# An attention block and a routed expert block: matrix slices over eight batches, the last attention step in a new order, and the end in whole loads and halves

## The reference, cut to what matters

```python
x = x + _layernorm(_L0_attn_ref(_layernorm(x), Wq, Wk, Wv, Wo, gamma, beta))
x = x + _layernorm(_L0_ffn_ref(_layernorm(x), router_w, w1, w2))
...
probs = softmax(xt @ router_w)
top_p, top_i = top_k(probs, 2)
for e in range(8):
    gate_e = sum(where(top_i == e, top_p, 0.0))
    hidden = gelu(xt @ w1[e])
    out = out + gate_e[:, None] * (hidden @ w2[e])
```

## Time and profile before

| | |
|---|---|
| median of 3 runs | 724.96 us (724.06 to 725.15) |
| profiled execution | 728.19 us, span 726.4 us |
| PE busy | 685.2 us, 94% |
| DVE busy | 554.1 us, 76% |
| ACT busy | 520.7 us, 72% |
| POOL busy | 273.6 us, 38% |
| DMA | 34.88 MB |

### The profile page before, as it was taken

How to read it: one execution, slowest core, us unless ns; L and a number is a source line. 1 busy time by engine, 2 the same in 40 slices (tenths; PEclk the granted TensorE clock), 3 DMA queues, 4 the chain that set the end, 5 groups by cost and what they waited for, 6 DMA issues and landing times.

```text
span 726.4 us, 17681 instructions
## 1 busy us (share of the span) xinstructions
PE 685.2 (94%) x5954; PEld 592.6 (82%) x5955; DVE 554.1 (76%) x1914; ACT 520.7 (72%) x1687; POOL 273.6 (38%) x388
## 2 busy tenths in 40 slices
PE   4999999999999999999999999999989999999954
PEld 3788878888888888888888888888869989999921
DVE  5668889888898989888898989888896774444226
ACT  4787877887888778887788878888774665555415
POOL 3023534232323132332323232332313777655535
PEclk9999999999999999999999999999989999999978
DMA  9630000010000000000000000000020243322155
GB/s 160 205 80 8 9 9 16 17 30 10 23 9 24 9 24 12 22 23 17 23 9 24 9 23 12 20 24 9 17 69 20 71 124 112 90 79 79 39 190 171
DMA packets 43701, 34.88 MB, mean 48 GB/s; under 512 B 10624, under 2 KB 40320, under 8 KB 43616
## 3 DMA queue, kind: packets, MB, share of 16 engines
q1 hardware_dynamic: 37984, 23.81, 12.8%
q0 software_dynamic: 4544, 9.45, 3.6%
q10 hardware_dynamic: 1088, 0.54, 0.3%
HBM read 20.22 MB, written 13.56 MB: 47 GB/s over the span
## 4 chain that ended last, share of the span: by engine, by line
PE 78%; DVE 12%; DMA 3%; ACT 2%; issue 2%; DVEq 1%; POOL 1%; SPq 0%; POOLq 0%; ACTq 0%
PE PT1O L423 11%; PE M L683 9%; PE SC L406 8%; PE A L434 6%; PE M L385 5%; PE M L387 5%; PE M L386 5%; PE SC L414 4%; PE PT1O L442 3%; PE SC L409 3%; PE PT L447 3%; PE PT L446 3%; PE SC L385 3%; PE SC L386 2%; PE SC L387 2%
## 5 line engine op out<-in xcount | busy, mean ns | idle before, releaser
L1262 ACT ACTIVATE qk<-M 128x512 f32<-128x512 f32 x127 | 76.0, 599 | 84.5 <-PE M L387 84.5
L1273 ACT ACTIVATE prob<-SC,nmax 128x256 f32<-128x256 f32 x256 | 126.0, 492 | 0.0
L423 PE MATMUL PT1O<-pT,v_sb 128*64 128x256 f32 (+1 forms) x1024 | 98.6, 335 | 0.7 <-ACT pT L1278 0.7
L423 PEld LDWEIGHTS PT1O<-pT,v_sb 128*64 128x64 f32 x1024 | 64.0, 138 | 43.0 <-ACT pT L1278 17.4
L1267 ACT ACTIVATE prob<-SC,nmax 128x128 f32<-128x128 f32 x256 | 95.6, 383 | 3.4 <-DVE nmax L777 3.3
L1543 POOL DMA_INDIRECT expert_rows<-v_sb,got x78 | 76.8, 984 | 47.0 <-ACT v_sb L1417 25.9
L787 DVE TENSOR_TENSOR prob<-prob,rden 128x512 f32<-128x512 f32 x128 | 88.8, 694 | 2.4 <-DVE rden L781 0.2
L1532 POOL DMA_INDIRECT sent_rows<-rec,slot x64 | 66.6, 1040 | 57.7 <-DVE slot L1037 39.2
L777 DVE TENSOR_REDUCE nmax<-SC 128x2 f32<-128x512 f32 x128 | 86.9, 679 | 0.0
L385 PE MATMUL M<-xt_hi,wqk_hi 128*128 128x256 f32 x254 | 82.5, 325 | 3.0 <-DVE xt_lo L771 2.2
L406 PE MATMUL SC<-qk 64*128 64x256 f32 x512 | 83.9, 404 | 0.6 <-ACT prob L1273 0.6
(11 more groups left out here) (189 smaller groups left out, 1782.1 us busy)
## 6 DMA issues: line engine op xcount, KB each, us to landing
got<-sent_rows SPq DMA_DIRECT2D x39, 132.0 KB, 2.3
w_in<-expert_rows SPq DMA_DIRECT2D x16, 256.0 KB, 3.7
x_in<-L_attn_x SPq DMA_DIRECT2D x16, 128.0 KB, 2.2
w_in<-L_ffn_w SPq DMA_DIRECT2D x1, 2048.0 KB, 13.6
x_res<-L_attn_x SPq DMA_DIRECT2D x16, 128.0 KB, 2.1
w_sb<-L_ffn_w SPq DMA_DIRECT2D x8, 256.0 KB, 4.3
out<-y_out SPq DMA_DIRECT2D x8, 256.0 KB, 2.1
sent_rows<-pad_rec SPq DMA_DIRECT2D x11, 132.0 KB, 4.6
```

Source lines behind the costliest of these rows:

```text
L423: last = mm(PT1O[k * E:(k + 1) * E, cols], v_sb[:, t, h * E:(h + 1) * E], src[:, par, k, :], start=(t == 0), stop=(t == 1), skip_group_che ...
L1273: return a.activation(prob[:, slot, k, 1:3, :].rearrange("p n t -> p (n t)"), SC[par][:, k, LATE_Q], ACT.Exp, bias=nmax[:, par, 0, k:k + 1 ...
```

## The change

- `split_w1` works in 32 slices of 128 columns, one a step in batches 1 to 8, each behind the masks of its step; it was 16 slices of 256 columns in batches 1 and 2, each behind a projection.
- At the start, TensorE runs 13 and 6 matmuls that nobody reads around the first transposes (`keep_busy`), the projection waits for each half of the low parts by itself, GpSimd's memsets wait for `wv_ok`, the second input is loaded ahead of `wo`, TensorE waits for `wo` in the third step, and VectorE clears the tables there (`tables_cleared`).
- In the last attention step the early table stands right behind the router's part 4, and TensorE transposes the first two tiles ahead of the second pair's probabilities. `last_pairs` has a new order too; `router(B - 3, 5)` and `finish(B - 2)` move into it, `router(B - 2, 0)` behind tile 0.
- For the last batch `dispatch` is cut in `find_places` and `send_places`; `late_table` parts move by half a turn; pads are issued a turn earlier; the store of tile 8 is issued behind `send(B - 1)`.
- The last two tiles are gated and stored in halves, with a PSUM bank for each half.
- At the end, the row numbers (`ids`) are laid out so that a group is one load of 4 KB a partition; nine matmuls that nobody reads run ahead of the sums; the first and the last group are worked in halves (`PARTS`, ten parts); there are eight PSUM banks and four places for moments and outputs, which were two.

```diff
-    back_groups = back[0:K * N, :].rearrange("(r g b p t) d -> r g p b t d", r=K, g=NG, p=P, t=T)
+    back_groups = back[0:K * N, :].rearrange("(g p r k) d -> g p r k d", g=NG, p=P, r=K)
...
+        PARTS = [(g, h * GT // 2, GT // 2) if g in (0, NG - 1) else (g, 0, GT)
+                 for g in range(NG) for h in range(2) if h == 0 or g in (0, NG - 1)]
...
-        W1_BATCHES = 2
-        W1_SLICE = NE * F // (NP * W1_BATCHES)
+        W1_BATCHES = 8
+        W1_SLICE = NE * F // (STEPS * W1_BATCHES)
...
-        sum_bank = (SC[0][:, 0], SC[0][:, 1], SC[1][:, 0], SC[1][:, 1])
+        last_banks = M, A
+        sum_bank = (SC[0][:, 0], SC[0][:, 1], SC[1][:, 0], SC[1][:, 1], M, A, PT1O, PT0)
...
             load_qk(1)
+            sp.wait_ge(sem("xn_done"), 1)
+            sp.dma_start(x_in[:], x_tiles[1]).then_inc(sem("x_in_ld"), 16)
             sp.dma_start(wo_sb[:], wo.rearrange("(c p) d -> p c d", p=P)).then_inc(sem("wo_ld"), 16)
...
-                for r in range(K):
-                    sp.dma_start(zz[:, g % 4, r].rearrange("p (b t) d -> p b t d", t=T), back_groups[r, g]).then_inc(zz_ld[g % 4], 16)
+                sp.dma_start(zz[:, g % 4], back_groups[g]).then_inc(zz_ld[g % 4], 16)
...
+            def keep_busy(dst, n):
+
+                for _ in range(n):
+                    mm(dst[:, 0:S], ident_bf[:], mask[:].rearrange("p n t -> p (n t)"), start=True, stop=True,
+                       skip_group_check=True)
+
             pe.wait_ge(sem("ident_ok"), 1)
+            pe.wait_ge(sem("mask_ok"), 1)
+            keep_busy(PT0, 13)
             x_transpose(0, M)
+            keep_busy(PT0, 6)
...
                     w_o((c - 4) % NP)
+                    if is_last(b) and u == STEPS - 1:
+
+                        w_o((c - 3) % NP)
+                        first_rows()
...
                 for t in range(2):
                     for c in range(NF):
-                        last = mm(out_bank[:, t * D:(t + 1) * D], hidT[:, s, c, t * P:(t + 1) * P],
-                                  w2_e[:, c * D:(c + 1) * D], start=(t == 0 and c == 0), stop=(c == NF - 1),
+                        last = mm((last_banks[t] if parted else out_bank)[:, t * D:(t + 1) * D], hidT[:, s, c, t * P:(t + 1) * P],
+                                  w2_e[:, c * D:(c + 1) * D], start=((t == 0 or parted) and c == 0), stop=(c == NF - 1),
                                   skip_group_check=True)
-                last.then_inc(sem("out_mm"), 1)
+                    if t == 1 or parted:
+                        last.then_inc(sem("out_mm"), 1)
...
+            for _ in range(9):
+                mm(PT0[:], ident[:], wo_sb[:, 0:4].rearrange("p c d -> p (c d)"), start=True, stop=True, skip_group_check=True)
...
+                if is_last(b) and u == STEPS - 1:
+
+                    expert_weights(0, w1_at[0])
+                    pT1_copy(p - 1)
+                    maxima(p + 1)
+
+                    dve.wait_ge(sem("gT_mm"), 2)
+                    split_rows(0, 0, M[:, 0:ROWS])
+                    expert_weights(1, w1_at[1])
+                    reciprocals(p)
+                    normalise_pair(p)
+                    return
...
+                    if is_last(b):
+                        early_table(5)
+                        w1_at[:] = experts(0, 2)
...
                 if n == 10:
+                    router(B - 1, 6)
+                    send_places(B - 1)
                     late_table(0)
-                    late_table(1)
...
                 if n == 9:
-                    router(B - 1, 6)
                     counts_copy(B - 1, False)
-                    dispatch(B - 1)
+                    find_places(B - 1)
...
+            def gated_halves(n, k):
+                act.wait_ge(back_st[k], 32 * (n // RING))
+                for t in range(2):
+                    act.wait_ge(sem("out_mm"), halves_done(n, t))
+                    a.activation(yo[:, k, t, :], last_banks[t][:, t * D:(t + 1) * D], ACT.Copy,
+                                 scale=got[:, k, t, C_GATE:C_GATE + 1]).then_inc(sem("yo_done"), 1)
...
             inverse_root("x", T, ln_eps, 1)
 
+
+            pool.wait_ge(sem("wv_ok"), 1)
             q.memset(ones_bf[:], 1.0)
...
+                n = STEPS * (b - 1) + u
+                if n == 0:
                     pool.wait_ge(sem("w1_ld"), 16)
...
+                cs = slice(n * W1_SLICE, (n + 1) * W1_SLICE)
+                pool.wait_ge(s_mm, NP * b + 2 * u + 1)
+                q.tensor_copy(w1_hi_f[:, cs], w1_in_f[:, cs]).then_inc(sem("w1_h"), 1)
...
             send(B - 2, [1])
-            early_stores(7, 9)
+            early_stores(7, 8)
 
             send(B - 1)
-            early_stores(9, EARLY)
+            early_stores(8, EARLY)
```

More of the change, by code:

```diff
@@ L297, in batch @@
             def batch(b):
-                if there(b, -1) and there(b):
+                if there(b, -1) and there(b, 1):
                     sp.wait_ge(sem("xn_done"), b + 1)
@@ L537, in step @@
                     p_transpose(p - 1)
-                if k >= 2:
+                if k >= 2 and not (is_last(b) and u == STEPS - 1):
                     w_o((c - 3) % NP)
@@ L850, in step @@
                         finish(b - 1)
-                    if there(b, 2) and not is_last(b):
+                    if there(b, 2):
                         router(b - 2, 5)
-                if is_last(b) and u == STEPS - 1:
-                    dve.wait_ge(sem("gT_mm"), 2)
-                    split_rows(0, 0, M[:, 0:ROWS])
                 reciprocals(p)
                 normalise_pair(p)
+                if first:
+                    x_stats(1)
+                if b == 0 and u == 2:
+                    tables_cleared()
                 if u == 0:
@@ L878, in step @@
                         x_stats(b + 2)
-                    if there(b, 2) and not is_last(b):
+                    if there(b, 2):
                         router(b - 2, 6)
-                if is_last(b) and u == 2:
-                    router(b - 2, 5)
                 if is_last(b + 1) and u == 3:
@@ L1401, in store_pads, with gelu @@
                         .then_inc(sem("pad_st"), 16)
-            def gelu(n, s):
-                for u in range(2):
+            def gelu(n, s, halves=range(2)):
+                for u in halves:
                     act.wait_ge(sem("up_mm"), 2 * n + u + 1)
@@ L1609, in _ @@
             for n in range(TILES - 2, TILES):
[L1610 to L1617 removed]
+                store_halves(n, n % RING)
+            for n, (g, first, size) in enumerate(PARTS):
+                o = f"o{n % 4}"
+                pool.wait_ge(sem("mv_o"), n + 1)
+                q.tensor_tensor(ve[o][:, 0:size], mv[o][:, 0:size, 1], ln_eps[:, 0:size], ALU.add).then_inc(sem("ve_o"), 1)
+                pool.wait_ge(sem("ve_o"), n + 1)
+                q.tensor_tensor(rstd[o][:, 0:size], ve[o][:, 0:size], half[:, 0:size], ALU.pow).then_inc(sem("rstd_o"), 1)
 _INS = ["L0_attn_x", "L0_attn_Wq", "L0_attn_Wk", "L0_attn_Wv", "L0_attn_Wo", "L0_attn_gamma", "L0_attn_beta",
```

263 lines of the change are left out of this document (141 added, 122 removed).

## The result

The changed kernel takes 715.35 us in the median of four runs (714.67 to 716.46), and the kernel before 725.06 on the same chip (724.06 to 726.01): a ratio of 0.9868, with a 95% interval of 0.9848 to 0.9887. It is 9.7 us faster, where I forecast 17.6. The profiled executions stand further apart: 728.19 us before, 715.87 after, 12.3 us.

The account below looks back on a forecast made before the run. TensorE has most work, so only fewer matmuls or waits help; five places add: 3.1 + 2.0 + 4.0 + 1.6 + 6.9 = 17.6 us, giving 710.6 profiled and 707.4 in the median, range 702.5 to 713.

Parts of the forecast that it names:

- Start: Up to the first masked scores: memsets moved off the input normalisations, then the `wv` load sets the pace; 3.1 us gained.
- Slices: First expert weights split over eight batches: batch 2 credited 2.3 us, 0.3 taken off for 24 new slices; 2.0 us.
- rival of colliding slices: Batches 3 to 8: GpSimd's slices still meet VectorE's multiplications and delay TensorE; time 713.5 us, chance 0.13.
- Last attention step: Earlier table and tile rows give 2.7 us, the less fallen TensorE clock 1.3; 4.0 us in all.
- Hence 2.7 us at least pass through the 12.67: Last attention step: a table 2.7 us earlier brings the first down projection, 12.67 us behind the landed rows, equally forward.
- I subtract the sum from both: Whole kernel: the summed gain is taken from the profiled execution, 728.19 us, and from the median, 724.96.
- First 16 tiles: Two TensorE waits in the first 16 expert tiles: 1.1 us at tile 10, 0.5 of 0.9 at tile 14; 1.6 us.
- I credit 1.1: Tile 10: TensorE's 1.09 us loss goes, since VectorE's wait for the dispatch's stores now stands behind `split_rows`.
- End: Behind the last expert tile: earlier last store, first statistics 4.2 us earlier, shorter way to the last addition; 6.9 us.
- with the same 2.75 behind it: End: the execution lasts 2.75 us beyond the last addition as before, ending at 719.5 instead of 726.4.
- the end gains little: End: loads of 4 KB pieces come no sooner or the nine matmuls overrun; end gives 3.0, time 711.3, chance 0.10.
- More than forecast: No clock fall in the last step (another 1.5), start 3.7, end 8.2; time 703 us or below, chance 0.09.

Follow-up runs that it names:

- a_root_act: Changed kernel with the inverse roots of the last two half groups taken from GpSimd, made by ScalarE and VectorE: 714.49 us, before 726.36, ratio 0.9833.
- after_again: The changed kernel, unchanged, run again on a slow chip for a second profile: 747.40 us, before 751.62.
- a_old16_2: Changed kernel with the turns of the first 16 tiles as before, second run: 715.56 us, before 726.36, ratio 0.9857.
- a_pool_late: Changed kernel with one more GpSimd instruction, a memset that waits for the last output addition: 717.64 us, before 726.36, ratio 0.9886.
- a_old16: Changed kernel with the turns of the first 16 tiles as before, on a slow chip: 748.88 us, before 757.69, ratio 0.9861.

## Why the prediction was wrong

The sign was right and the size was not: the range (702.5 to 713) missed 715.35. By the terms of the sum, in the profiled executions:

- **Start**: 3.1 forecast, 3.35 measured. The mechanism (memsets gone from under `xn`, then `wv`'s landing) is as told.
- **Slices**: 2.0 forecast, 3.1 measured. Batch 2 gave 2.2 of the 2.3 credited. The rest is a term that the sum lacked: the other batch with slices, batch 1, gave 0.9. The row nearest to the new place, 32.7 for a batch with no slices, was the right bound: the 24 slices cost 0.2. The rule of the Trainium skill, page "SBUF — State Buffer", section "Who interferes with whom", leaves a reduction from PSUM untouched; the trace agrees, 32.9 against 32.9 us a batch. Of VectorE's multiplications of the probabilities seven took over 0.75 us before and one (0.96) now. The rival of colliding slices fell.
- **Last attention step**: 4.0 forecast, 3.75 measured in the profile and 1.3 between other executions, on slow chips. That the profile came near the forecast is luck. The first step that failed is "Hence 2.7 us at least pass through the 12.67". The table did come 2.8 us earlier as counted from the last `xt_st` (41.1 us behind it instead of 43.9), but in the kernel before the 12.67 us behind the load held 6.8 us at half clock (539.05 to 545.87), up to 3.4 us lost; in the changed kernel, all at the high clock, the stretch from the tiles' first transposes (529.84) to the down projection is still 12.55. There TensorE no longer waits for the rows but for VectorE's and ScalarE's parts of the last pairs (0.62, 0.69 and 0.73 us). So nearly all of the 3.75 is the clock's, and an earlier table gives some 0.6 (an estimate: 3.75 less 3.1). The second is "I subtract the sum from both": the profiled execution of before was 3.2 us above its median, for which that fall of the clock is the one cause that the traces show, and a sum that takes part of its gain from the fall can't be taken from the median. 12.3 between the profiles less 3.1 (728.19 − 725.06) and plus 0.5 (715.87 − 715.35) is the 9.7 of the medians.
- **First 16 tiles**: 1.6 forecast, −1.7 in the profile. The step that failed is "I credit 1.1". The wait at tile 10 did go, but behind it stands the load of tile 16, whose time the last batch's dispatch sets and not TensorE: TensorE waited 1.86 us there instead of 0.9. The 0.5 credited to earlier pads was the second error: before, the last pad did land last, as I had read, but the last dispatch store only 0.19 us ahead of it. The clock's fall behind the longer wait cost another 1.5 where it came, and no term held it.
- **End**: 6.9 forecast, 4.0 measured. Of its pieces, the halves gave 1.1 as forecast and the first statistics came 3.6 closer instead of 4.2 (each landing to sum 0.14 longer, not 0.3 shorter). From there to the last addition it takes 19.5 instead of 18.3: VectorE's work is 16.2 and not 15.6, since half groups cost an aggregate, a shift and a wait for GpSimd each, and TensorE's sums pace the first 2.6 us. The step that failed most plainly is "with the same 2.75 behind it": that tail was GpSimd's drain, level with the output's landing before, and it came out from under it when the outputs became shorter. The tail is 1.1 longer, and 1.7 longer than the 2.15 that `a_root_act` has without the drain.

Of the rivals, "the end gains little" (3.0, time 711.3) was the nearest, and it had a chance of 0.10 for another reason, late loads. In "More than forecast" the sum is off: 707.4 less 1.5, 0.6 and 1.3 is 704.0 and not 703, which lies inside the forecast's own 703 to 711. Most signs I had named for a right forecast came: masks at 11.8, intervals of 32.0 to 33.1 (31.7 in the first), the down projection 10 us earlier, clock at 1.00 in the first sums. Those that failed told: a short wait for tile 16's load, first statistics 4.2 us closer, and VectorE nearly without gaps (16.2 us of work in 19.5).

The 0.5 credited to tile 16's load, the 1.1 at tile 10, the 2.7 of the earlier table and the 2.75 behind the last addition are one kind of error: something that ended last was moved, and I didn't ask what arrives at the same place next.

## What to carry to other kernels

Before a profile's sum is taken from a median, compare the granted clock of the profiled execution with that of the others: what a fall of the clock cost in one execution is no gain in the rest. When a wait is removed, look for the next thing that TensorE needs and what sets its time; if TensorE doesn't set it, the wait only moves. Look at the last 6 us of the trace engine by engine, drains too: GpSimd's last operation should, by these 20 traces, lie 5.2 us ahead of the point where the outputs have landed, so its small work near the end belongs on another engine.

## What I had not expected of the hardware

GpSimd's final drain ended 4.99 to 5.16 us behind its last operation in all 20 profiles, also behind a memset of 0.10 us (5.14).

The same wait of TensorE, 1.9 to 2.7 us for tile 16's load, was followed by a low clock for 3.4 us in two profiles (waits of 1.86 us in the changed kernel and 2.14 in `a_root_act`) and by none in two others (2.04 in `a_old16_2` and 2.74 in `a_pool_late`).

On three chips the kernel before took 751 to 758 us instead of 725. There VectorE's wait behind the logits ended 1.8 us after the matmul that frees it (320.48 against 318.72 in `after_again`), against 0.04 on the first chip; six batches of that profile and ten of one of the kernel with the new end have such a wait, 2.6 us long. In the first 16 tiles engines stood up to 6.5 us (VectorE in `a_old16`) with nothing in the trace that they waited for. What these chips do differently stays open.
